# Second attention of a two-layer block: another order of the steps on TensorE, over three rotating pairs of banks

## Chip, cores and metric

The kernel runs on one core of one Trainium2 chip. The metric is the time of one execution on the device, in microseconds; smaller is better.

## What is computed

The reference chains two layers over an image tensor of 2 x 256 x 32 x 32 in float32. The first is a deformable attention with a position bias from a small network, an output projection and a two-layer network with GELU. The second, the one that matters here, is a plain attention of 8 heads of 32 channels over the N = 1024 pixels of each of the 2 images:

```python
xf = jnp.transpose(x.reshape(B, C, N), (0, 2, 1))
qkv = (xf @ W_qkv + b_qkv).reshape(B, N, N_HEADS, 3 * D_K)
q, k, v = jnp.split(qkv, 3, axis=-1)
attn = jnp.einsum('bihd,bjhd->bijh', q, k) * SCALE
attn = jax.nn.softmax(attn, axis=2)            # over j
res = jnp.einsum('bijh,bjhd->bihd', attn, v).reshape(B, N, N_HEADS * D_K)
res = res @ W_out + b_out + xf
```

## The kernel before

Five engine programs run side by side and meet by semaphores that count finished steps. The last fifth of the span is the second layer. It has G = 16 heads (two images of eight) and each head has NK = 8 tiles of 128 pixels, so there are SLOTS = 128 units. A unit goes through these steps:

- `along(x)` (L1041 to L1056, matmuls at L1055) on TensorE: the scores of 128 queries against all 1024 keys, queries on the partitions. Two matmuls of 512 columns fill one pair of PSUM banks. VectorE's `maxes(x)` (L760) takes the maximum of each query from it; `mx_ready` counts these.
- `turn(n)` (L1066): when the eight maxima of head n are there, one transpose lays them along the free axis. ScalarE (L572) and VectorE (L765) split the result in a high and a low part (`m_hi`, `m_lo`), and SP moves them by DMA (L330) as two more rows of the queries (`m_in`).
- `across(s)` (matmuls at L1083): the scores again, keys on the partitions and with the maximum subtracted by the two extra rows. It fills another pair of banks. ScalarE takes the exponential of it (L588) into one of six buffers; `pr_ready` counts these, `st_ready` the finished `across`.
- `weigh(s)` (L1094): the weighted sum of the values, in column-tiled matmuls of 32 columns of weights each, four side by side, into bank 6 or 7.
- GpSimd (L434) adds the exponentials of two units; `sums(j)` (L1104) sums such a pair over the partitions with column-tiled matmuls. `added` and `sums_done` count these.
- VectorE inverts the sums (L774, four pieces of a head) and divides (L782); SP places the head (L338).

`along` runs AHEAD_MAX = 14 units ahead of `across`: iteration s of the mixed loop has `along(s + 14)`. Three heads of queries and keys are held (HEADS3). The queries of head n + 3 are requested by ScalarE (L551) behind the exponential of unit 8n + 7, the last that reads that buffer, and `along` waits for them in `st_in` at its first tile. The keys are requested by SP (L324) at the same point.

`across(s)`, `along(x)` and `turn(n)` share six banks as three pairs, and a writer may only start when the pair's last reader is done. The functions `along_pair`, `turn_pair` and `across_pair` say which pair a step takes; `turned(x)` counts the transposes that stand before unit x, since each takes a turn in the rotation, and `turning(x)` says that one stands right there. `x` is always the unit of `along`, `s` that of `across`, x = s + 14.

In the mixed loop the order of one iteration before is

```python
if turning(x): turn(turned(x) - 1)
along(x); across(s); weigh(s - 2)
if s % 2 == 1 and s >= 5: sums((s - 5) // 2)
```

so two units are along, across, weigh, along, across, weigh, sums. The first 14 `along` stand ahead of the loop, among the projections of the values, and the last 14 iterations have none: those are called the tail. Behind the loop come the output projection and the stores.

Of the kernel before, what the change touches and what calls it, by code (L numbers as in the profile page):

```python
# [13 lines left out]
G = B * NH  # L14
# [8 lines left out]
NK = N // P  # L23
# [20 lines left out]
HEADS3, PRING, AHEAD_MAX = 3, 6, 14  # L44
# [3 lines left out]
SLOTS = G * NK  # L48
# [11 lines left out]
def build(nc, d, out):  # L60
# [5 lines left out]
    with ctx:  # L66
# [3 lines left out]
        def sem(name):  # L70
            return ctx.enter_context(nc.semaphore(name))
# [82 lines left out]
        def bank(i, n=1):  # L154
            return ps[:, 512 * i:512 * (i + n)]
# [5 lines left out]
        def v(name, i=0, n=1):  # L161
# [35 lines left out]
        tr_ready, m_hi, m_lo, m_in, ones_ready, bo_ready, bo_saved = (  # L197
            sem(x) for x in ("tr_ready", "m_hi", "m_lo", "m_in", "ones_ready", "bo_ready", "bo_saved"))
        sc_ready, mx_ready, st_ready, pr_ready, pv_done, o_done = (
            sem(x) for x in ("sc_ready", "mx_ready", "st_ready", "pr_ready", "pv_done", "o_done"))  # L200
# [20 lines left out]
        TURN = NK + TURN_LAG  # L221

        def turning(x):

            return TURN <= x < TURN + SLOTS and (x - TURN) % NK == 0

        def turned(x):

            return min(max((x - TURN) // NK + 1, 0), G)

        def along_pair(x):

            return (x + turned(x)) % 2 if x < AHEAD_MAX else (2 * (x - AHEAD_MAX) + turned(x) - 1) % 3

        def turn_pair(n):

            x = TURN + NK * n
            return x % 2 if x < AHEAD_MAX else (2 * (x - AHEAD_MAX) + n - 1) % 3

        def across_pair(s):  # L240

            return (2 * s + turned(s + AHEAD_MAX)) % 3

        block = ctx.enter_context(nc.Block())

# [192 lines left out]
        def _(act):  # L438
# [142 lines left out]
            for s in range(SLOTS):  # L581
                if turning(s + AHEAD_MAX):
                    max_high(turned(s + AHEAD_MAX) - 1)
                act.wait_ge(st_ready, s + 1)
                if s >= PRING:
                    act.wait_ge(pv_done, s - PRING + 1)
                    act.wait_ge(added, (s - PRING) // 2 + 1)
                act.activation(PT[s % PRING], bank(2 * across_pair(s), 2), ACT.Exp).then_inc(pr_ready, 1)  # L588
                if s % NK == NK - 1 and HEADS3 <= s // NK + 3 < G:
                    load_queries(s // NK + 3)  # L590
# [3 lines left out]
        def _(dve):  # L594
# [159 lines left out]
            def maxes(x):  # L754

                n, it = x // NK, x % NK
                dve.wait_ge(sc_ready, x + 1)
                if it == 0 and n >= HEADS3:
                    dve.wait_ge(tr_ready, n - HEADS3 + 1)
                dve.tensor_reduce(amax[n % HEADS3][:, it:it + 1], bank(2 * along_pair(x), 2), AX.X, ALU.max, negate=True).then_inc(mx_ready, 1)  # L760
# [51 lines left out]
        def _(pe):  # L812
# [98 lines left out]
            for m in range(PAIRS * G + AHEADQ):  # L911
# [7 lines left out]
                n = m - AHEADQ + 1  # L919
# [58 lines left out]
            for n in range(T):  # L978
                b, hf = n // 2, n % 2
                for ct in range(CT):  # L980
                    r = CT * n + ct
# [8 lines left out]
            for n in range(T):  # L990
                b, hf = n // 2, n % 2
                pe.wait_ge(xn2_ready, CT * (n + 1))
                for f in range(FT):
                    r = FT * n + f
# [6 lines left out]
                for ct in range(CT):  # L1001
                    r = CT * n + ct
# [38 lines left out]
            def along(x):  # L1041

                n, it = x // NK, x % NK
                if it == 0:
                    pe.wait_ge(st_in[n % HEADS3], 96 * (n // HEADS3 + 1))
                if 2 <= x < AHEAD_MAX and not turning(x - 1):
                    pe.wait_ge(mx_ready, x if turning(x) else x - 1)
                elif turning(x) or x == AHEAD_MAX:
                    pe.wait_ge(mx_ready, x)
                elif turning(x - 1):  # L1050
                    pe.wait_ge(m_lo, turned(x))
                elif x >= AHEAD_MAX + 2:
                    pe.wait_ge(pr_ready, x - AHEAD_MAX - 1)
                for hf in range(2):
                    last = pe.matmul(bank(2 * along_pair(x) + hf), QS[n % HEADS3][0:ROWS, P * it:P * (it + 1)],  # L1055
                                     KS[n % HEADS3][0:ROWS, HALF * hf:HALF * (hf + 1)], start=True, stop=True)  # L1056
                last.then_inc(sc_ready, 1)

            def turn(n):

                pe.wait_ge(mx_ready, NK * (n + 1))
                if n > 0:
                    pe.wait_ge(pr_ready, TURN + NK * n - AHEAD_MAX - 1)
                else:
                    pe.wait_ge(mx_ready, TURN - 1)
                pe.transpose(bank(2 * turn_pair(n))[0:NK, 0:P], amax[n % HEADS3][:, :], ident[:, :]).then_inc(tr_ready, 1)  # L1066

            def across(s):

                n, kt = s // NK, s % NK  # L1070
                if kt == 0:
                    pe.wait_ge(m_in, 32 * (n + 1))
                x = s + AHEAD_MAX
                if turning(x):
                    pe.wait_ge(pr_ready, s)
                elif x <= SLOTS:
                    pe.wait_ge(mx_ready, x - (s == 0))
                else:
                    pe.wait_ge(pr_ready, s - 2)
                    if x - 2 == TURN + NK * (G - 1):  # L1080
                        pe.wait_ge(m_lo, G)
                for hf in range(2):
                    last = pe.matmul(bank(2 * across_pair(s) + hf), KS[n % HEADS3][0:ROWS + 2, P * kt:P * (kt + 1)],  # L1083
                                     QS[n % HEADS3][0:ROWS + 2, HALF * hf:HALF * (hf + 1)], start=True, stop=True)
                last.then_inc(st_ready, 1)

            def weigh(s):

                n, kt = s // NK, s % NK
                if kt == 0 and n >= 2:  # L1090
                    pe.wait_ge(o_done, n - 1)
                pe.wait_ge(pr_ready, s + 1)
                for c in range(4):
                    last = pe.matmul(bank(6 + n % 2)[D * c:D * (c + 1), 0:QUARTER], V[:, n, kt, :],  # L1094
                                     PT[s % PRING][:, QUARTER * c:QUARTER * (c + 1)],
                                     start=(kt == 0), stop=(kt == NK - 1), skip_group_check=True)
                last.then_inc(pv_done, 1)

            def sums(j):

                n = j // (NK // 2)
                pe.wait_ge(added, j + 1)
                for c in range(4):
                    last = pe.matmul(bank(6 + n % 2)[D * c:D * (c + 1), QUARTER:2 * QUARTER], ones[:, :],  # L1104
                                     PSUMS[j % 2][:, QUARTER * c:QUARTER * (c + 1)],
                                     start=False, stop=(j % (NK // 2) == NK // 2 - 1), skip_group_check=True)
                last.then_inc(sums_done, 1)
# [3 lines left out]
            for n in range(2 * NK):  # L1111
                value(n)
                x = n - 2
                if turning(x):
                    turn(0)
                if x >= 0:
                    along(x)
            pe.wait_ge(vv_saved, 2 * NK)
            pe.wait_ge(ones_ready, 1 + HEADS3)
            for s in range(SLOTS + 4):  # L1120
                x = s + AHEAD_MAX
                if turning(x):
                    turn(turned(x) - 1)
                if x < SLOTS:
                    along(x)
                if s < SLOTS:
                    across(s)
                if 0 <= s - 2 < SLOTS:
                    weigh(s - 2)
                if s % 2 == 1 and s >= 5:  # L1130
                    sums((s - 5) // 2)

            pe.wait_ge(mx_ready, SLOTS)
            pe.wait_ge(pr_ready, SLOTS)
# [70 lines left out]
```

## Time and profile before

| | us |
|---|---|
| median of 3 runs | 1362.77 (1358.43 to 1364.05) |
| profiled execution | 1364.95 |
| its span | 1363.2 |
| TensorE busy | 1258.7 (92%) |
| VectorE busy | 807.5 (59%) |
| ScalarE busy | 815.0 (60%) |
| GpSimd busy | 694.4 (51%) |

The rows of the trace are those of one profiled execution. A row of the timeline gives the start of an instruction from the start of the span, its duration, engine, source line, operation, output and input; equal instructions that follow each other are merged (x8). PE is TensorE's matmuls, PEld its weight loads, DVE is VectorE, ACT ScalarE, POOL GpSimd, SPq and ACTq the DMA issues of SP and ScalarE. In square brackets stands the idle time of the engine before the row and what ended it. Ends of matmuls are modelled, so the distances between starts are the safer reading.

### The profile page before, as it was taken

How to read it: one execution, taken by the hardware profiler on the slowest of the kernel's cores; microseconds unless marked ns; L12 is line 12 of the kernel's file. 1: busy time of each engine (PE TensorE's matmuls, PEld its weight loads, DVE VectorE, ACT ScalarE, POOL GpSimd, SP SyncE). 2: the span in 40 equal slices, each digit the busy share in tenths (PEclk: the TensorE clock that was granted, in tenths of full speed). 3: DMA queues.
4: the chain of work that ended last, by engine and by line, in shares of the span. 5: the costliest groups of instructions: out<-in, count | busy, mean ns of one | idle time of the engine just before them, and what ended most of it. 6: DMA issues, size and time to landing. Idle time of an engine off the chain costs nothing.

```text
span 1363.2 us, 24765 instructions
## 1 busy us (share of the span) xinstructions
PE 1258.7 (92%) x10364; PEld 484.7 (36%) x10364; DVE 807.5 (59%) x954; ACT 815.0 (60%) x899; POOL 694.4 (51%) x363
## 2 busy tenths in 40 slices
PE   4159999999999999999999999879999899999998
PEld 2132222222222222222222223634444644444443
DVE  6876666666666666666666665730002667777773
ACT  3378777777777777777777775442212344555552
POOL 4076666666666666666666663320000055565564
PEclk9579999999999999999999999989999989999999
DMA  2141101110110011011101100000005222222212
GB/s 71 41 148 32 32 1 32 32 32 2 32 32 21 13 32 32 2 32 32 32 1 32 32 1 1 1 0 0 0 0 206 110 49 54 58 57 56 56 33 74
DMA packets 21842, 51.40 MB, mean 38 GB/s; under 512 B 5394, under 2 KB 10258, under 8 KB 21572
## 3 DMA queue, kind: packets, MB, share of 16 engines
q1 hardware_dynamic: 19424, 43.53, 11.9%
q10 hardware_dynamic: 2308, 6.30, 1.8%
q8 instruction: 82, 1.34, 0.4%
q14 instruction: 28, 0.23, 0.1%
HBM read 36.63 MB, written 10.95 MB: 35 GB/s over the span
## 4 chain that ended last, share of the span: by engine, by line
PE 85%; DMA 5%; DVE 4%; POOL 2%; ACT 2%; issue 1%; ACTq 1%; SPq 0%; POOLq 0%; DVEq 0%
PE ps L892 32%; PE ps L901 17%; PE ps L883 5%; PE ps L1055 5%; PE ps L998 4%; PE ps L1008 4%; PE ps L1083 4%; PE ps L1094 4%; DMA h1h<-q_d 3%; DVE big L636 2%; PE ps L1027 2%; DMA qk<-q_d 1%; PE ps L1104 1%; POOL big L394 1%; PE ps L1037 1%; PE ps L985 1%
## 5 line engine op out<-in xcount | busy, mean ns | idle before, releaser
L892 PE MATMUL ps<-big,w 64*64 64x512 f32 x4096 | 483.3, 588 | 0.0
L503 ACT ACTIVATE big<-ps 128x1024 f32<-128x1024 f32 x256 | 262.1, 1024 | 178.7 <-PE ps L892 178.7
L690 DVE TENSOR_SCALAR big<-big 128x1024 f32<-128x1024 f32 x256 | 177.8, 695 | 263.8 <-POOL big L409 263.8
L684 DVE TENSOR_TENSOR big<-qpad,ps 128x1024 f32<-128x1024 f32 x256 | 311.1, 1215 | 7.9 <-ACT ps L482 5.4
L409 POOL TENSOR_TENSOR big<-qpad 128x1024 f32<-128x1024 f32 x128 | 244.7, 1911 | 133.1 <-PE ps L892 69.4
L409 POOL TENSOR_TENSOR big<-qpad,V 128x1024 f32<-128x1024 f32 x128 | 244.5, 1910 | 129.6 <-PE ps L892 73.4
L503 ACT ACTIVATE big<-ps,vec 128x1024 f32<-128x1024 f32 x256 | 284.1, 1110 | 0.0
L901 PE MATMUL ps<-big,w3s 128*32 128x512 f32 x2048 | 246.2, 598 | 1.3 <-ACT big L503 1.3
L892 PEld LDWEIGHTS ps<-big,w 64*64 64x64 f32 x4096 | 146.5, 133 | 205.9 <-issue 112.6
L588 ACT ACTIVATE big<-ps 128x1024 f32<-128x1024 f32 x128 | 131.1, 1024 | 117.3 <-PE ps L1083 117.2
L434 POOL TENSOR_TENSOR big<-big 128x1024 f32<-128x1024 f32 x32 | 76.1, 2378 | 232.0 <-ACT big L588 232.0
L760 DVE TENSOR_REDUCE amax<-ps 128x1 f32<-128x1024 f32 x128 | 156.4, 1222 | 59.7 <-PE ps L1055 56.0
L901 PEld LDWEIGHTS ps<-big,w3s 128*32 128x32 f32 x2048 | 53.4, 109 | 181.8 <-ACT big L503 92.2
L434 POOL TENSOR_TENSOR BT<-big 128x1024 f32<-128x1024 f32 x32 | 76.3, 2383 | 59.5 <-ACT big L588 49.6
L883 PE MATMUL ps<-S,wl 57*64 57x512 bf16 x1024 | 102.1, 389 | 1.5 <-ACT vs L498 1.5
L1094 PE MATMUL ps<-big 128*32 128x256 f32 x1024 | 82.9, 397 | 0.0
L883 PEld LDWEIGHTS ps<-S,wl 57*64 57x64 bf16 x1024 | 29.5, 105 | 144.7 <-ACT big L503 80.7
L1055 PE MATMUL ps<-h1l,h1h 96*128 96x512 f32 x176 | 67.0, 463 | 10.9 <-DMA h1h<-q_d 9.1
L752 DVE SCALAR_TENSOR_TENSOR X<-ps,vec,X 128x512 f32<-128x512 f32 x8 | 6.0, 751 | 105.0 <-PE ps L1008 105.0
L544 ACT ACTIVATE big<-ps,vec 128x512 f32<-128x512 f32 x32 | 22.0, 689 | 73.0 <-PE ps L998 73.0
L1083 PE MATMUL ps<-h1h,h1l 98*128 98x512 f32 x176 | 57.2, 406 | 0.4 <-DVE amax L760 0.4
L998 PE MATMUL ps<-XN,m 128*128 128x512 f32 x128 | 55.7, 593 | 0.8 <-DVE X L743 0.8
(146 smaller groups left out, 988.4 us busy)
## 6 DMA issues: line engine op xcount, KB each, us to landing
raw<-s_f SPq DMA_DIRECT2D x32, 512.0 KB, 6.2
h1l<-k_d SPq DMA_DIRECT2D x33, 128.0 KB, 3.6
h1h<-q_d ACTq DMA_DIRECT2D x33, 128.0 KB, 4.1
X<-in_x SPq DMA_DIRECT2D x2, 1024.0 KB, 6.1
q_d<-XN SPq DMA_DIRECT2D x4, 512.0 KB, 3.6
k_d<-XN SPq DMA_DIRECT2D x4, 512.0 KB, 4.1
q_d<-big SPq DMA_DIRECT2D x4, 512.0 KB, 4.0
k_d<-big SPq DMA_DIRECT2D x4, 512.0 KB, 5.3
```

What stands on the lines that cost most here:

```text
L409: pool.tensor_tensor(h1[m % HRING].rearrange("p (y a b) -> p y a b", y=2, b=W), u.unsqueeze(2).to_broadcast(shape), a[:, :, HALF // W * hf ...
L434: pool.tensor_tensor(PSUMS[j % 2], PT[2 * j % PRING], PT[(2 * j + 1) % PRING], ALU.add).then_inc(added, 1)
L503: act.activation(h2[m % H2RING], z2[m % ZRING], ACT.Relu, bias=v("cb2") if m % 2 else 0.0).then_inc(h2_ready, 1)
L588: act.activation(PT[s % PRING], bank(2 * across_pair(s), 2), ACT.Exp).then_inc(pr_ready, 1)
L684: dve.tensor_tensor(h1[m % HRING].rearrange("p (y a b) -> p y a b", y=2, b=W), u.unsqueeze(2).to_broadcast(shape), b[:, :, HALF // W * hf: ...
L690: dve.tensor_scalar(h1[m % HRING], h1[m % HRING], 0.0, None, ALU.max).then_inc(h1_ready, 1)
L760: dve.tensor_reduce(amax[n % HEADS3][:, it:it + 1], bank(2 * along_pair(x), 2), AX.X, ALU.max, negate=True).then_inc(mx_ready, 1)
L883: pe.matmul(z2[m % ZRING][CH * y:CH * (y + 1), HALF * x:HALF * (x + 1)], wl1[CH * x:CH * x + KROWS, 2 * w + y, :], S[CH * x:CH * x + KROWS ...
L892: last = pe.matmul(z2[m % ZRING][CH * y:CH * (y + 1), HALF * x:HALF * (x + 1)], w2[CH * x:CH * (x + 1), :], h1[m % HRING][CH * x:CH * (x + ...
L901: last = pe.matmul(zb[32 * k:32 * (k + 1), :], w3s[:, a:a + 32], h2[(m + k // 2) % H2RING][:, HALF * (k % 2):HALF * (k % 2 + 1)], start=(m ...
L1055: last = pe.matmul(bank(2 * along_pair(x) + hf), QS[n % HEADS3][0:ROWS, P * it:P * (it + 1)], KS[n % HEADS3][0:ROWS, HALF * hf:HALF * (hf ...
L1094: last = pe.matmul(bank(6 + n % 2)[D * c:D * (c + 1), 0:QUARTER], V[:, n, kt, :], PT[s % PRING][:, QUARTER * c:QUARTER * (c + 1)], start=( ...
```

## The change

On TensorE the mixed loop runs in rounds of two units. A round is across, along, across, along, then both weighs of the round before, then the sums of the round before that. `across` now stands ahead of `along` in each unit, and the transpose ahead of both. The rotation over the three pairs follows the new order: the steps of a round take pairs c - 1, c, c + 1 and c + 2, which is c - 1 again. The waits in `along`, `turn` and `across` are rewritten to fit; the matmuls, the buffers, and the programs of the other four engines stay as they are, but for the pair from which they read.

```diff
         def along_pair(x):
 
-            return (x + turned(x)) % 2 if x < AHEAD_MAX else (2 * (x - AHEAD_MAX) + turned(x) - 1) % 3
+            if x < AHEAD_MAX:
+                return (x + turned(x)) % 2
+            s = x - AHEAD_MAX
+            return (4 * (s // 2) + 2 * (s % 2) + turned(x)) % 3
...
         def across_pair(s):
 
-            return (2 * s + turned(s + AHEAD_MAX)) % 3
+            return (4 * (s // 2) + 2 * (s % 2) + turned(s + AHEAD_MAX) - 1) % 3
...
                 if 2 <= x < AHEAD_MAX and not turning(x - 1):
                     pe.wait_ge(mx_ready, x if turning(x) else x - 1)
-                elif turning(x) or x == AHEAD_MAX:
+                elif 2 <= x < AHEAD_MAX:
+                    pe.wait_ge(m_lo, 1)
+                elif x < 2:
+                    pass
+                elif turning(x):
                     pe.wait_ge(mx_ready, x)
-                elif turning(x - 1):
-                    pe.wait_ge(m_lo, turned(x))
-                elif x >= AHEAD_MAX + 2:
-                    pe.wait_ge(pr_ready, x - AHEAD_MAX - 1)
+                elif x == AHEAD_MAX:
+                    pe.wait_ge(mx_ready, x - 1)
+                else:
+                    pe.wait_ge(pr_ready, x - AHEAD_MAX)
...
                 pe.wait_ge(mx_ready, NK * (n + 1))
-                if n > 0:
-                    pe.wait_ge(pr_ready, TURN + NK * n - AHEAD_MAX - 1)
+                if n < G - 1:
+                    pe.wait_ge(mx_ready, TURN + NK * n - 1)
                 else:
-                    pe.wait_ge(mx_ready, TURN - 1)
+                    pe.wait_ge(pr_ready, TURN + NK * n - AHEAD_MAX - 2)
...
                 if turning(x):
                     pe.wait_ge(pr_ready, s)
-                elif x <= SLOTS:
-                    pe.wait_ge(mx_ready, x - (s == 0))
-                else:
+                elif turning(x - 1):
+                    pe.wait_ge(m_lo, turned(x))
+                elif s == 0:
+                    pe.wait_ge(mx_ready, AHEAD_MAX)
+                elif s > 1 and x - 1 <= SLOTS:
+                    pe.wait_ge(mx_ready, x - 1)
+                elif s > 1:
                     pe.wait_ge(pr_ready, s - 2)
-                    if x - 2 == TURN + NK * (G - 1):
-                        pe.wait_ge(m_lo, G)
...
-            for s in range(SLOTS + 4):
-                x = s + AHEAD_MAX
-                if turning(x):
-                    turn(turned(x) - 1)
-                if x < SLOTS:
-                    along(x)
-                if s < SLOTS:
-                    across(s)
-                if 0 <= s - 2 < SLOTS:
-                    weigh(s - 2)
-                if s % 2 == 1 and s >= 5:
-                    sums((s - 5) // 2)
+            for r in range(SLOTS // 2 + 2):
+                for s in (2 * r, 2 * r + 1):
+                    x = s + AHEAD_MAX
+                    if turning(x):
+                        turn(turned(x) - 1)
+                    if s < SLOTS:
+                        across(s)
+                    if x < SLOTS:
+                        along(x)
+                if 0 < r <= SLOTS // 2:
+                    weigh(2 * r - 2)
+                    weigh(2 * r - 1)
+                if r >= 2:
+                    sums(r - 2)
```

## Rows read from the trace of the kernel before

**Rows 1.** Busy time by engine, with granted clock, DMA share, rate: mixed loop with `along`.

```profile
core 0: us, PE busy (x) PEld busy (x) DVE busy (x) ACT busy (x) POOL busy (x), PEclk, DMA share, GB/s
1086.45:1322.26 235.81, 222.10 (x1807) 110.91 (x1807) 170.63 (x193) 120.28 (x128) 133.33 (x56) 0.98 0.23 52
```

**Rows 2.** Timeline, two units in the middle of the loop.

```profile
1216.78 0.73 PE L1055 MATMUL ps<-h1l,h1h 96*128 96x512 f32 x2
...
1217.36 0.63 PE L1083 MATMUL ps<-h1h,h1l 98*128 98x512 f32 x2
1217.55 1.22 DVE L760 TENSOR_REDUCE amax<-ps 128x1 f32<-128x1024 f32 x1 [0.44 <-PE ps L1055]
...
1217.91 0.64 PE L1094 MATMUL ps<-big 128*32 128x256 f32 x8
...
1218.48 0.73 PE L1055 MATMUL ps<-h1l,h1h 96*128 96x512 f32 x2
1218.70 0.55 DVE L774 RECIPROCAL big<-ps 128x64 f32<-128x64 f32 x1
...
1220.06 0.61 PE L1104 MATMUL ps<-BT,ones 128*32 128x256 f32 x8
...
1220.61 0.73 PE L1055 MATMUL ps<-h1l,h1h 96*128 96x512 f32 x2
```

**Rows 3.** Waits, 1090 to 1322: who waited for whom, total us, times, longest.

```profile
PE ps L1055 <- DMA h1h<-q_d: 9.1, 9, 1.6
...
PE ps L1055 <- DMA qk<-q_d: 4.1, 4, 1.2
```

**Rows 4.** Busy time of two stretches, columns as in rows 1.

```profile
1107.20:1114.00 6.80, 6.80 (x34) 3.13 (x33) 3.01 (x4) 2.32 (x3) 1.66 (x1) 0.50 0.00 0
1127.70:1131.10 3.40, 3.40 (x24) 1.72 (x20) 1.48 (x2) 1.55 (x2) 0.00 (x0) 0.51 0.00 0
```

**Rows 5.** Timeline, the third pair of units, and the tail.

```profile
1092.90 0.73 PE L1055 MATMUL ps<-qk 96*128 96x512 f32 x2
...
1323.49 0.73 PE L1083 MATMUL ps<-qk 98*128 98x512 f32 x2
...
1324.15 0.64 PE L1094 MATMUL ps<-big 128*32 128x256 f32 x8
1324.26 1.02 ACT L588 ACTIVATE big<-ps 128x1024 f32<-128x1024 f32 x1 [0.20 <-PE ps L1083]
...
1342.59 1.05 PE L1094 MATMUL ps<-big 128*32 128x256 f32 x16
...
1343.45 0.61 PE L1104 MATMUL ps<-big,ones 128*32 128x256 f32 x8
```

**Rows 6.** Timeline, steps that had to wait, and what released them.

```profile
1088.49 0.73 PE L1083 MATMUL ps<-h1h,h1l 98*128 98x512 f32 x2 [0.39 <-DVE amax L760]
...
1089.06 0.62 PE L1055 MATMUL ps<-qk 96*128 96x512 f32 x2
...
1211.59 1.23 DVE L760 TENSOR_REDUCE amax<-ps 128x1 f32<-128x1024 f32 x1 [0.49 <-PE ps L1055]
...
1212.96 0.08 PEld L1066 LDWEIGHTS ps<-ident,amax 128*8 128x8 f32 x1 [0.41 <-DVE amax L760]
...
1341.81 1.02 ACT L588 ACTIVATE big<-ps 128x1024 f32<-128x1024 f32 x1 [0.21 <-PE ps L1083]
...
1342.88 0.27 PEld L1094 LDWEIGHTS ps<-big 128*32 128x32 f32 x8 [0.16 <-ACT big L588]
```

**Rows 7.** Timeline, requests of queries and the `along` that waited for them.

```profile
1099.66 1.31 ACTq L551 DMA_DIRECT2D h1h<-q_d  x3
...
1106.08 0.73 PE L1055 MATMUL ps<-h1l,h1h 96*128 96x512 f32 x2 [1.64 <-DMA h1h<-q_d]
...
1125.97 0.73 PE L1055 MATMUL ps<-h1l,h1h 96*128 96x512 f32 x2 [1.45 <-DMA h1h<-q_d]
...
1203.56 1.30 ACTq L551 DMA_DIRECT2D h1h<-q_d  x3
...
1209.10 0.74 PE L1055 MATMUL ps<-h1l,h1h 96*128 96x512 f32 x2 [0.76 <-DMA h1h<-q_d]
```

## Prediction

> **What bounds the kernel now.** I first cut the span into stages. The change touches only the second attention, from the first step of its mixed loop to the end of the loop. [Rows 1] gives the part in which `along` still runs, 235.81 us: TensorE is busy 222.10 us, VectorE 170.63, ScalarE 120.28, GpSimd 133.33. So TensorE is the candidate, and the timeline of two units shows how it spends its time [rows 2]: `along` at 1216.78, `across` at 1217.36, `weigh` at 1217.91, `along` at 1218.48, `across` 0.57 later, and after the second `weigh` the `sums` at 1220.06 and the next `along` at 1220.61. Each step starts about 0.57 us after the one before, sums 0.45 and the step after sums 0.55; two units take 1220.61 - 1216.78 = 3.83 us, with nothing idle. TensorE's own order of instructions is the limit there.
>
> Then the waits of that stretch [rows 3]: `along` waited 13 times, once for each head from the fourth on, for the DMA of its queries, 9.1 + 4.1 = 13.2 us of idle TensorE. Third, the granted clock [rows 4]: two stretches, 6.8 us and 3.4 us long, at 0.50 and 0.51, that is at 1.2 GHz instead of 2.4. Each begins one to two microseconds after one of the two longest DMA waits, and the clock was 2.4 GHz before it.
>
> These close the account: first two rounds 1092.90 - 1086.45 = 6.45 us [rows 1, 5], then 55 rounds x 3.83 = 210.65, DMA waits 13.2, together 230.3; measured 235.8. The remaining 5.5 us is the low clock, half of its 10.2 us or 5.1, and 0.4 for getting under way after the waits. After 1322.26 seven rounds without `along` remain.
>
> **Part 1: the order on TensorE.** The same matmuls are issued; only their neighbours change. Rows show what a neighbour is worth. A pair of 512-column matmuls that stands alone between column-tiled groups takes 1324.15 - 1323.49 = 0.66 us [rows 5]; two pairs together take 1217.91 - 1216.78 = 1.13 [rows 2], which is 0.47 for the second. So a run of full-width matmuls pays 0.19 once. For `weigh` and `sums`: alone 0.57 [rows 2], one after another 0.43 (two weighs and then the sums, 1343.45 - 1342.59 = 0.86 for two) [rows 5]: 0.14 once per run. Before, two units hold two runs of each kind; after, one of each. Four pairs take 1.13 + 2 x 0.47 = 2.07, weigh, weigh and sums 0.45 + 0.43 + 0.55 = 1.43, the round 3.50. Against 3.83 this would be 0.33 less, if nothing waits.
>
> The Trainium skill, "TensorEngine Tiling (Array Packing)", Tiling Modes, says that a change of tiling mode drains the engine; it gives no price. The rows above give it, 0.19 + 0.14 = 0.33 for a run of each kind.
>
> **Part 2: the wait that it adds.** Three pairs of banks now serve four writers in a round, so the second `along` takes the pair that the first `across` of the same round has just filled: it waits until ScalarE has exponentiated it (pr_ready at s + 1). Before, `along` needed only the exponential of two units back. From the start of a first-in-run `across`, the exponential starts at 1324.26 - 1323.49 = 0.77 [rows 5] and takes 1.02; the trace has no `along` that waits for it, so I bound the wake-up by the nearest rows [rows 6]: weights for ScalarE's result start at 1342.88, 0.05 after 1341.81 + 1.02; the transpose starts 0.14 after VectorE's 1211.59 + 1.23. I take 0.05, the row with the same engine pair. So the second `along` starts at 0.77 + 1.02 + 0.05 = 1.84, where TensorE would have reached it at 0.57 + 2 x 0.47 = 1.51: a stall of 0.33. After a wait the run begins anew: at 1088.49 `across` was released by VectorE and the next step came 0.57 later, not 0.47 [rows 6]; so this `along` costs the full 0.66. Queued behind it are both weighs, the sums and the next `across`. The round is 1.84 + 0.66 + 1.43 = **3.93 us**, 0.10 more than before: the wait eats all that the order gives. 55 rounds: **+5.5 us** (with 0.14 for the wake-up +10.5; with the weight load hidden, -0.1 a round, 0).
>
> That last end has a page too. The Trainium skill, "TensorE: Matmul & The Clock Gate", Architectural detail, says the queue can pull weight loads ahead of matmuls in flight. By that the sum would be some 5 us lower. The 0.57 at 1088.49 speaks against it where the load itself carries the wait.
>
> Nobody else becomes late. A maximum starts 0.77 after a first-in-run `along` [rows 2], 0.10 less further in the run, as there the weights are loaded beforehand. The first of a round starts at 1.24 and ends at 2.47; a reciprocal of 0.55 [rows 2] may follow; the second ends by 4.25, and the third step of the next round, at 4.97, is the first that needs it. The second exponential runs from 1.80, when ScalarE is free, to near 2.87; the sum on GpSimd, which is busy 133 us of the 236, has more than a round from there until `sums` reads it, as before.
>
> **Part 3: the DMA wait.** The queries of head n+3 are issued when exponential 8n+7 starts: 1203.56, and `along` could go at 1209.10, 5.5 us; in the worst case 1099.66 to 1106.08, 6.4 [rows 7]. Before, that issue came 0.89 before the end of a round (0.67 into the last `across`, which starts at 1218.48 + 0.57 = 1219.05, 1.56 before 1220.61) and the `along` opened the round after the next one: 0.89 + 3.83 = 4.7 us, short by 0.8 to 1.7. Now `across` of unit 8n+7 is third in its round and its exponential starts when the previous one ends, at 1.80; the `along` is second in the round after next, at 2 x 3.93 + 0.57 = 8.4. There are 6.6 us for a transfer of 5.5 to 6.4. The wait goes in all 13 places: **-13.2 us**, and -0.4 for the restarts. Next late there is nothing: the keys go out on SP at the same moment, behind the move of the maxima; `across` of a new head comes 0.3 us earlier after its transpose (7.9 for 8.2), and two rounds of only 2.9 in the tail of before passed with no DMA wait.
>
> **Part 4: the clock.** Both low stretches follow waits of 1.64 and 1.45 us [rows 7]; after the 11 others, (13.2 - 3.1) / 11 = 0.9 us each, there is none. With these gone I take the clock back: **-5.1 us**; if not, up to 5.1 stays.
>
> **Part 5: start and tail.** At the start `across` goes first and waits for the same maximum as `along` did; following the same durations round 2 begins 0.4 us earlier. `across` now stands before `along` behind m_in, but the first head's maxima leave some 6 us before. Tail: seven rounds of 1.13 + 1.43 = 2.56 instead of 0.66 + 0.57 + 0.66 + 1.00 = 2.89: -2.3; the last transpose's `across` waits there for the exponential just before it (ends at 2.87 of a 2.56 round): +0.4. Together **-2.3**.
>
> **Sum.** +5.5 - 13.2 - 0.4 - 5.1 - 2.3 = -15.5. The profiled execution took 1364.95 (span 1363.2), so 1349.4; it lies 2.2 above the median of the runs, 1362.77. The prediction is 1362.8 - 15.5 = **1347.3 us**.
>
> **Rivals.**
> 1. *The bubble turns the clock down (slower).* The new stall of 0.33 us stands in every round, where the old one came once a head. If 15 stretches of 3.4 us at 1.2 GHz follow, half of that or 1.7 us each, that adds 26 to the 5.1 not saved: 1347.3 + 5.1 + 26 = 1378. It passes +0.5% (1369.6) from 11 stretches on. Against it: TensorE would idle 0.33 of 3.93 us, 8%; a round with one of the 11 shorter DMA waits idled 0.9 of 4.8, 19%, and kept its clock [rows 2 to 4]. Chance 0.06. The Trainium skill, "TensorE: Matmul & The Clock Gate", A second HAM failure mode, describes just this: short idling between groups that cycle through PSUM banks makes the clock swing. The present trace has no such case.
> 2. *The DMA wait stays.* If the queries' landing hangs on something that moves with the loop (contention, the keys), 13.6 us stay: about 1361. For it: landing varies, 5.5 to 6.4, with 0.2 to spare in the worst case. Chance 0.06.
> 3. *The exponential's wait costs nothing*, because the pair is free earlier than the records say: rounds of 3.50, 55 x 0.43 = 24 us less: 1323. Against it: in [rows 6] the waiting instruction starts after its releaser's record ends. Chance 0.04.
> 4. *The forecast*, 0.84. Its own ends: weight load hidden, -5.5, 1342; wake-up 0.14 and half the clock loss kept, +5 + 2.6, 1355.
>
> **Range** 1338 to 1359, which holds the forecast with its ends and leaves out most of the rivals, some 0.17. Half a per cent, about what a measurement of this kernel can tell from no change, is 6.8 us: faster means below 1356. Nearly all of case 4 and case 3: 0.84; same, rival 2 and the upper edge of 4: 0.10; slower, rival 1: 0.06.
>
> **What the profile would show.** A round of 3.93 us with `along` in it, the second `along` released by ScalarE with 0.3 us idle or a little more, 57 times; no DMA row among TensorE's waits; a granted clock of 1.00 from 1090 on. Wrong would be: rounds of 3.5 (rival 3), a clock below 1.00 in many stretches (1), DMA waits at the heads (2), or a maximum of VectorE as the releaser of `across`, which my account says never comes.

## The result and the profile after

The changed kernel takes 1348.93 us (median of 6 runs, 1347.46 to 1351.33) against 1361.4 us for the kernel before (6 runs, 1357.19 to 1364.05); the ratio is 0.9908 with a 95% interval of 0.9887 to 0.9928, that is 9.8 to 15.4 us less. The forecast was 1347.3. The profiled execution took 1349.23 us, its span is 1347.4, against 1364.95 and 1363.2 before. It is faster by more than half a per cent, and by the mechanism forecast; one term, that of the clock, was too large.

The chain that ended last, first before, then after (share of the span by engine):

```profile
PE 85%; DMA 5%; DVE 4%; POOL 2%; ACT 2%; issue 1%; ACTq 1%; SPq 0%; POOLq 0%; DVEq 0%
```

```profile
PE 86%; ACT 6%; DVE 4%; POOL 2%; issue 1%; DMA 1%; ACTq 0%; SPq 0%; POOLq 0%; DVEq 0%
```

DMA has all but left the chain and ScalarE has come in: one wait was exchanged for another. The next rows give the busy time by engine, with granted clock, DMA share and rate, of the mixed loop with `along` (it answers to rows 1), and then of the tail up to the output projection:

```profile
core 0: us, PE busy (x) PEld busy (x) DVE busy (x) ACT busy (x) POOL busy (x), PEclk, DMA share, GB/s
1085.69:1308.56 222.87, 212.61 (x1806) 113.69 (x1806) 166.70 (x193) 115.44 (x128) 133.52 (x56) 1.00 0.24 55
1308.56:1330.20 21.64, 20.34 (x234) 10.39 (x230) 4.62 (x11) 13.85 (x15) 19.05 (x8) 1.00 0.08 20
```

The loop fell from 235.81 to 222.87 us, 12.9 less, at a granted clock of 1.00 throughout. The tail fell by 2.0, from 1345.92 - 1322.26 = 23.66 to 21.64. Another 0.8 us lies before the loop, where nothing was changed.

One round of two units after (it answers to rows 2; lines 1062, 1092, 1103 and 1113 are `along`, `across`, `weigh` and `sums`):

```profile
1206.06 0.73 PE L1092 MATMUL ps<-h1h,h1l 98*128 98x512 f32 x2
...
1206.62 0.64 PE L1062 MATMUL ps<-h1l,h1h 96*128 96x512 f32 x2
1206.82 1.97 ACT L591 ACTIVATE big<-ps 128x1024 f32<-128x1024 f32 x2 [1.99 <-PE ps L1092]
...
1207.10 0.63 PE L1092 MATMUL ps<-h1h,h1l 98*128 98x512 f32 x2
...
1207.77 1.30 ACTq L554 DMA_DIRECT2D h1h<-q_d  x3
...
1207.90 0.73 PE L1062 MATMUL ps<-h1l,h1h 96*128 96x512 f32 x2 [0.17 <-ACT big L591]
...
1208.56 1.07 PE L1103 MATMUL ps<-big 128*32 128x256 f32 x16
...
1209.45 0.61 PE L1113 MATMUL ps<-BT,ones 128*32 128x256 f32 x8
...
1209.99 0.73 PE L1092 MATMUL ps<-qk 98*128 98x512 f32 x2
```

The round is 1209.99 - 1206.06 = 3.93 us. Counted from its start, the exponential starts at 0.76, the second `along` at 1.84, the weighs at 2.50, the sums at 3.39. The waits of TensorE over the loop were these (who waited for whom, total us, times, longest; it answers to rows 3):

```profile
PE ps L1062 <- ACT big L591: 9.9, 55, 0.2
PE ps L1092 <- DVE amax L763: 0.2, 1, 0.2
```

No DMA is among them. The 13 waits for queries are gone, and 55 short ones for the exponential stand instead. They show as 0.17 us each, because the modelled end of the matmul before hides the rest of the gap: against the 1.51 at which TensorE would have reached the step without a wait, the delay is 1.84 - 1.51 = 0.33.

### The profile page after: what moved, and what is told of

Read it like the earlier page. It is cut to its first block, busy times and chain, and to the rows that moved or that the text cites. A ratio compares the mean times of both kernels' runs of the same rounds, so it can differ in the third digit from the quotient of the medians.

```text
span 1347.4 us, 24764 instructions
## 1 busy us (share of the span) xinstructions
PE 1246.8 (93%) x10364; PEld 488.4 (36%) x10364; DVE 803.2 (60%) x954; ACT 808.8 (60%) x899; POOL 694.1 (52%) x363
## 4 chain that ended last, share of the span: by engine, by line
PE 86%; ACT 6%; DVE 4%; POOL 2%; issue 1%; DMA 1%; ACTq 0%; SPq 0%; POOLq 0%; DVEq 0%
PE ps L895 33%; PE ps L904 18%; PE ps L886 5%; PE ps L1103 5%; ACT big L591 4%; PE ps L1001 4%; PE ps L1011 4%; PE ps L1062 4%; PE ps L1092 3%; DVE big L639 2%; PE ps L1113 2%; PE ps L1030 2%; POOL big L397 1%; PE ps L1040 1%; PE ps L988 1%; PE ps L1154 1%
## 5 line engine op out<-in xcount | busy, mean ns | idle before, releaser
L506 ACT ACTIVATE big<-ps 128x1024 f32<-128x1024 f32 x256 | 262.0, 1023 | 179.1 <-PE ps L895 179.1
L591 ACT ACTIVATE big<-ps 128x1024 f32<-128x1024 f32 x128 | 125.3, 1024 | 91.7 <-PE ps L1092 91.7
L1062 PE MATMUL ps<-h1l,h1h 96*128 96x512 f32 x176 | 62.5, 437 | 6.9 <-ACT big L591 6.6
L1103 PE MATMUL ps<-big 128*32 128x256 f32 x1024 | 68.5, 385 | 0.0
```

Of the source, the lines that this page charges most:

```text
L506: act.activation(h2[m % H2RING], z2[m % ZRING], ACT.Relu, bias=v("cb2") if m % 2 else 0.0).then_inc(h2_ready, 1)
```

## The experiments

Times are medians; ratios are against the kernel before on the same chip, with 95% intervals. "Loop" is the time from the first matmul of the first `across` to the last matmul of the last `along`, read from the starts in the timeline. It leaves out the stages before and after, which vary by several us from run to run (over all the profiles the loop begins between 1085.3 and 1092.1 us). It is 233.4 us in the kernel before and 221.1 in the kernel after.

### Without the loads: what the DMA waits were worth

```diff
-                if HEADS3 <= n + 2 < G:
-                    sp.wait_ge(st_ready, NK * (n + 2 - HEADS3 + 1))
-                    load_keys(n + 2)
...
-                if s % NK == NK - 1 and HEADS3 <= s // NK + 3 < G:
-                    load_queries(s // NK + 3)
...
-                    pe.wait_ge(st_in[n % HEADS3], 96 * (n // HEADS3 + 1))
+                    pe.wait_ge(st_in[n % HEADS3], 96)
```

> The kernel before, with the loads of queries and keys from the fourth head on left out: later heads compute with the first three heads' data, so part of the computation is changed; the order on TensorE and every other wait stay. My theory says the DMA waits (13.2 us idle, 0.4 of restarts) and the low clock that follows the two longest (up to 5.1) went with the change: rounds stay at 3.83 us, the waits and the two low stretches vanish, 1343 to 1348 us. Rival, the gain came from the order of the matmuls and not from the DMA waits: 1358 to 1361.

Measured 1347.92 us, ratio 0.9885 (0.9853 to 0.9917), loop 217.2 us. Without its loads the old order is as fast as the new order with them. So the gain of the change is, on balance, the vanished DMA wait, not the order of the matmuls: in the loop the old order is even 3.9 us ahead (217.2 against 221.1), and the new one makes good 2.0 of that in the tail. Low clock was expected to be gone, but the 217.2 us hold one stretch of it at the start, where `along` and `across` wait for VectorE.

```profile
1088.00:1305.24 217.24, 216.86 (x1786) 109.11 (x1785) 169.01 (x192) 119.26 (x127) 132.88 (x56) 0.98 0.04 9
1090.00:1096.80 6.80, 6.80 (x28) 3.30 (x28) 3.16 (x4) 3.34 (x4) 3.02 (x2) 0.50 0.00 0
```

```profile
1087.46 0.70 PE L1050 MATMUL ps<-h1l,h1h 96*128 96x512 f32 x2 [1.41 <-DVE amax L755]
...
1089.48 0.79 PE L1078 MATMUL ps<-h1h,h1l 98*128 98x512 f32 x2 [0.38 <-DVE amax L755]
```

The wait of 1.41 us stands at the start of the loop in nine other traces too, the kernels before and after among them, and no low clock follows it in those.

### The critical exponential made shorter, and longer

```diff
-                act.activation(PT[s % PRING], bank(2 * across_pair(s), 2), ACT.Exp).then_inc(pr_ready, 1)
+                cols = N if s % 2 else HALF
+                act.activation(PT[s % PRING][:, 0:cols], bank(2 * across_pair(s), 2)[:, 0:cols], ACT.Exp).then_inc(pr_ready, 1)
```

> The kernel after, with the exponential of every even unit over the first 512 of its 1024 columns only (the other half of its weights is left out of the computation as such, old values stand there). My theory: the second along waits for exactly this exponential; shortened by some 0.4 us it ends at about 0.77 + 0.6 + 0.05 = 1.42 into the round, before TensorE wants the pair at 1.51, and the round falls from 3.93 to 3.50 us: 24 us less, about 1325. Rival, the order is worth less than the rows say and something else bounds the round (VectorE's maxima, GpSimd's sums): 1340 to 1349.

Measured 1328.19 us, ratio 0.9737 (0.9700 to 0.9773); loop 198.8, which is 22.3 us less than the kernel after, where 24 were expected. The median is 3 us above the 1325 expected. The loop accounts for 1.7 of them; the rest lies outside it (in this profile, of an execution of 1331.0, the loop began at 1089.8, 4 us later than in that of the kernel after). The timeline:

```profile
1205.95 0.73 PE L1093 MATMUL ps<-qk 98*128 98x512 f32 x2
...
1206.72 0.60 ACT L592 ACTIVATE big<-ps 128x512 f32<-128x512 f32 x1 [1.55 <-PE ps L1093]
...
1207.44 0.66 PE L1063 MATMUL ps<-h1l,h1h 96*128 96x512 f32 x2
...
1208.03 1.07 PE L1104 MATMUL ps<-big 128*32 128x256 f32 x16
...
1209.46 0.27 PE L1074 MATMUL ps<-ident,amax 128*8 128x128 f32 x1
```

The exponential is over at 1.37 of the round, the second `along` starts at 1.49 without a wait, and the next round (here with a transpose) begins after 3.51 us. That is the round of pure TensorE work, 3.50 in the prediction; neither VectorE nor GpSimd holds it up here.

The other way round:

```diff
+        spare, spared = sb("spare", [P, D]), sem("spared")
...
+                if s % 2 == 0:
+                    act.wait_ge(spared, s // 2)
+                    act.activation(spare[:, :], ident[:, 0:D], ACT.Exp).then_inc(spared, 1)
                 act.activation(PT[s % PRING], bank(2 * across_pair(s), 2), ACT.Exp).then_inc(pr_ready, 1)
```

> The kernel after, with one small activation (32 columns, some 0.1 to 0.25 us, read from the trace) put before the exponential of every even unit; nothing is left out. My theory: the round's chain is across, exponential, along, so each round with along grows by the whole of it: 57 times, +6 to +14 us, round 4.05 to 4.2. Rival, the exponential's wait is slack that something else fills: under +2 us.

```profile
1207.34 0.23 ACT L594 ACTIVATE spare<-ident 128x32 f32<-128x32 f32 x1 [0.20 <-PE ps L1096]
1207.48 1.92 ACT L595 ACTIVATE big<-ps 128x1024 f32<-128x1024 f32 x2
...
1208.54 0.73 PE L1066 MATMUL ps<-h1l,h1h 96*128 96x512 f32 x2 [0.30 <-ACT big L595]
```

Measured 1356.97 us, ratio 0.9944 (0.9922 to 0.9966); loop 227.7, 6.6 us more than the kernel after. The small activation pushes the exponential back by 0.14 (1207.34 to 1207.48), not by its own 0.23, since the two overlap; TensorE's wait grows from 0.17 to 0.30. 57 x 0.13 = 7.4 us against 6.6 in the loop, inside the 6 to 14 expected. The chain is as drawn, and there is no slack in it.

### The kernel before once more: how steady is the clock?

> The kernel before, unchanged, profiled once more. My theory: the DMA waits of about 1 us stand again at each head from the fourth on; whether the two stretches of low clock come again is open. If they are absent the time should be some 5 us lower, near the fastest runs of before (1357 to 1359); if they stand, 1362 to 1365.

Measured 1362.93 us, with 13 DMA waits again (13.6 us in all), loop 230.8. Of low clock there is one stretch instead of two:

```profile
1239.90:1243.30 3.40, 3.40 (x24) 1.76 (x20) 1.57 (x2) 1.64 (x2) 0.00 (x0) 0.50 0.00 0
```

It follows the one wait of 1.58 us; the twelve others were 0.81 to 1.38. So the low clock in this loop differs between runs of one kernel: 10.2 us in the first profile, 3.4 in this one. The loop is 2.6 us shorter than in the first profile and the profiled execution 2.0 us (1362.93 against 1364.95), so the stages outside it vary by as much as what was looked for. The executions without a trace point the same way: on one chip the kernel before ran 17 times, and the granted clock, averaged over the whole execution, goes with the time, from 0.976 in the fastest (1356.81 us) to 0.970 in the slowest (1364.63). In which stage their low clock lay is not recorded.

### Who stands first in the round

The kernel of this run makes its order of steps from a list; written in the loop of the kernel after, the change is:

```diff
-                    if s < SLOTS:
-                        across(s)
                     if x < SLOTS:
                         along(x)
+                    if s < SLOTS:
+                        across(s)
```

The three pairs go round in the order of the steps, and each step waits for the reader of the step three before it.

> Rounds of two units as in the kernel after, but along first: along, across, along, across, two weighs, sums, pairs and waits fitted. Nothing is left out. My theory: the fourth step takes the first step's pair, whose reader is now VectorE's maximum, 0.77 + 1.23 + 0.05 = 2.05 after the round's start instead of 1.84: round 2.05 + 0.66 + 1.43 = 4.14, 55 x 0.21 = 11.5 us more than the kernel after; the queries have some 5.5 us for 5.5 to 6.4, so DMA waits of 0 to 0.9 return, up to 12 us: 1360 to 1372. Rival, only the number of runs of each tiling mode counts, not who stands first: 1349.

Measured 1364.5 us, ratio 1.0017 (0.9997 to 1.0036), loop 234.7.

```profile
1204.52 0.73 PE L1126 MATMUL ps<-qk 96*128 96x512 f32 x2
...
1206.56 0.73 PE L1145 MATMUL ps<-h1h,h1l 98*128 98x512 f32 x2 [0.40 <-DVE amax L827]
1207.22 1.07 PE L1159 MATMUL ps<-big 128*32 128x256 f32 x16
```

The fourth step starts at 2.04 (forecast 2.05), released by VectorE. The matmuls are the same and stand in runs of the same length, yet the loop is 13.6 us longer than in the kernel after. That comes from which reader frees the pair of the fourth step, the exponential or the maximum (55 x 0.21 = 11.5), and from small DMA waits that return (6, 2.1 us in all). Rounds of two units by themselves give nothing.

### The same gain with one constant

AHEAD_MAX is 13 instead of 14 in the kernel before. The pairs and waits are derived from the order of the steps.

> The order of the kernel before (rounds of one unit, along first), with along 13 instead of 14 units ahead of across, and nothing left out. One unit more between the request of the queries and their use is 1.7 us, more than every wait seen but none above it. My theory: the DMA waits go, as in the run without the loads, at rounds of 3.83 us: 1346 to 1350, the whole gain of the change with a single constant. Rival, the shorter lead brings a wait for the moved maxima (5.4 us instead of 7.1 from transpose to across): 1355 to 1362.

Measured 1351.1 us, ratio 0.9918 (0.9892 to 0.9943), loop 221.4: about the kernel after's time, with the old order, and 1.1 us above what was expected. All DMA waits are gone and `across` never waits for the moved maxima. But the rounds with a transpose take 4.18 us instead of 3.84. The transpose now stands in the second unit of a round, with no `sums` ahead of it, and the `along` behind it takes the pair of the `along` before and waits for its maximum. It starts 0.36 after the transpose instead of 0.03:

```profile
1205.77 1.23 DVE L827 TENSOR_REDUCE amax<-ps 128x1 f32<-128x1024 f32 x1 [0.90 <-PE ps L1126]
...
1206.70 0.08 PEld L1136 LDWEIGHTS ps<-ident,amax 128*8 128x8 f32 x1 [0.41 <-issue]
...
1207.05 0.30 PEld L1126 LDWEIGHTS ps<-h1l,h1h 96*128 96x128 f32 x2 [0.27 <-DVE amax L827]
```

### How long the queries really take

```diff
-                if s % NK == NK - 1 and HEADS3 <= s // NK + 3 < G:
-                    load_queries(s // NK + 3)
+                if s % NK == 0 and s > 0 and HEADS3 <= s // NK + 2 < G:
+                    load_queries(s // NK + 2)
```

> The kernel after, with the queries of a head requested one exponential later (behind that of unit 8n+8 instead of 8n+7), nothing left out. My theory: 6.6 us of slack become 3.7, so the DMA wait comes back at 13 heads with 1.8 to 2.7 us each, 23 to 35 us; and waits as long as the two that were followed by a low clock are now the rule, so several stretches at 1.2 GHz, up to 1.7 us each, up to 22 us: 1372 to 1400. Rival for the clock, the low stretches have nothing to do with the wait's length: none or one or two in the loop, and 1372 to 1384.

Measured 1353.73 us in one run, with a loop of 221.1 us, the same as the kernel after to 0.1 us, and no DMA wait at all. My expectation failed. The timeline has the request of the queries at 1215.30, and the `along` that needs them, at 1219.03, follows the `across` at 1218.46 without a gap, 3.7 us after the request. The median time from an issue to its landing tells why. First the kernel before, then this one:

```profile
h1l<-k_d SPq DMA_DIRECT2D x27, 128.0 KB, 3.6
h1h<-q_d ACTq DMA_DIRECT2D x27, 128.0 KB, 4.1
```

```profile
h1l<-k_d SPq DMA_DIRECT2D x27, 128.0 KB, 2.6
h1h<-q_d ACTq DMA_DIRECT2D x27, 128.0 KB, 2.6
```

In the kernels before and after, the keys and queries of a head, three transfers of 128 KB each, are requested in the same moment from two queues and slow each other; here the keys go out 3.0 us ahead (1212.27). I tried this on the kernel before, by asking for the keys one `across` later:

```diff
-                    sp.wait_ge(st_ready, NK * (n + 2 - HEADS3 + 1))
+                    sp.wait_ge(st_ready, NK * (n + 2 - HEADS3 + 1) + 1)
```

> The kernel before, with the keys requested one across (1.7 us) later than the queries; nothing is left out. My theory after the run with late queries: keys and queries that are requested together slow each other from about 3.4 to 5.5 us until usable; apart, the queries are there after 3.4 and the keys 1.7 + 3.4 = 5.1 us after the same moment, with 4.7 available: waits of 0.4 instead of 1.0 us, 6 to 8 us less, 1353 to 1357. Rival, no contention, a transfer takes its 5.5 us whatever else runs: waits of 2.5 us, 20 us more and the low clock on top, 1380 and above.

Measured 1361.19 us, ratio 1.0005 (0.9990 to 1.0020), loop 229.4, waits 10.8 us instead of 13.2.

```profile
1200.68 1.25 ACTq L551 DMA_DIRECT2D h1h<-q_d  x3
...
1202.80 1.24 SPq L324 DMA_DIRECT2D h1l<-k_d  x3
...
1206.22 0.30 PEld L1055 LDWEIGHTS ps<-h1l,h1h 96*128 96x128 f32 x2 [1.24 <-DMA h1l<-k_d]
```

The mechanism holds, the gain does not, and the time is outside the 1353 to 1357 expected. Apart, the keys are usable 3.4 us after their request (1206.22 - 1202.80). But the next `across` comes 2.12 us later, not the 1.7 that I had taken, for a `sums` stands between; 2.12 + 3.4 is the same 5.5 as together. A transfer that took 5.5 us by itself would have made waits of some 3 us. The longest wait, 1.58 us at 1106.27, is again followed by 6.8 us at 1.2 GHz (1107.0 to 1113.8), against 10.2 us of low clock in the first profile of the kernel before; with the 2.4 us of waits that makes the 4.0 by which the loop is shorter.

### Long waits and the clock

Here the condition of the request is `s % NK == 2 and s > NK`, so that it goes out in the very round that needs the queries.

> The kernel after, with the queries requested behind the exponential of unit 8n+10, whose start is in the same round as the along that needs them; nothing is left out. In the run with the request one exponential late the transfer took 3.5 us or less from request to use. So TensorE must wait 0.77 + 3.4 - 0.57 = 3.6 us at each of 13 heads: 47 us. My theory of the clock (long waits are followed by 1.2 GHz): low stretches after most of these waits, 13 x 1.7 us or more, together 1410 to 1440. Rival (the low stretches of before were chance): none or one or two, 1394 to 1400.

Measured 1425.18 us in one run, loop 290.7. TensorE's waits, and three of the stretches of low clock that go with them:

```profile
PE ps L1062 <- DMA h1h<-q_d: 32.2, 9, 3.7
PE ps L1062 <- DMA qk<-q_d: 14.5, 4, 3.8
```

```profile
1113.10:1119.90 6.80, 5.86 (x32) 3.09 (x33) 2.45 (x2) 1.02 (x1) 0.03 (x1) 0.50 0.00 1
1137.00:1140.40 3.40, 3.40 (x27) 1.23 (x25) 2.12 (x2) 1.02 (x1) 0.00 (x0) 0.50 0.00 0
1345.20:1352.00 6.80, 6.80 (x34) 3.84 (x35) 2.73 (x3) 1.39 (x3) 1.12 (x1) 0.50 0.00 0
```

The waits add 46.7 us, as expected. Each of the 13 is attended by a fall to 1.2 GHz, four times for 6.8 us and nine times for 3.4, 57.8 us in all. Half of that, 28.9, and the 46.7 make 75.6; the loop grew by 290.7 - 221.1 = 69.6. Two things are likely to make the difference: some stretches begin in the wait itself (that at 1113.1 ends up beside a matmul only at 1114.04), and 13 fewer waits for the exponential stand in the list. After waits of this length the low clock is no chance. For shorter waits chance has a part, as the stretch in the run without the loads shows.

### The exponential in two halves, one per bank

The run with the half exponential named the price of the new wait, 22 us. It can be had without leaving anything out: split each exponential by bank, and let each matmul of the next writer wait for its own bank. In short form (the waits of `weigh` and of the other engines count in halves accordingly):

```diff
-                act.wait_ge(st_ready, s + 1)
+                act.wait_ge(st_ready, 2 * s + 1)
...
+                for hf in range(2):
+                    if hf == 1:
+                        act.wait_ge(st_ready, 2 * s + 2)
+                    act.activation(PT[s % PRING][:, HALF * hf:HALF * (hf + 1)], bank(2 * across_pair(s) + hf), ACT.Exp).then_inc(pr_ready, 1)
...
                 for hf in range(2):
+                    pe.wait_ge(pr_ready, 2 * p[1] + 1 + hf)     # p[1]: the across that filled this pair
                     last = pe.matmul(bank(2 * along_pair(x) + hf), ...
```

> The order of the kernel after, but every exponential in two halves of 512 columns, the first started when the first matmul of across is done, and the second along's first matmul waits for the first half only, its second matmul for the second half. Nothing is left out. My theory: the stall of the second along shrinks from 0.43 us (0.33 and the 0.10 of a new start) to 0.1 to 0.2, though ScalarE works 2 x 0.60 instead of 1.02 us: round 3.6 to 3.7, 13 to 18 us less than the kernel after, 1331 to 1336. Rival, the halves cost as much as they release: 1345 to 1352.

Measured 1326.23 us, ratio 0.9742 (0.9701 to 0.9782), loop 200.0: 5 us below the range expected.

```profile
1209.25 0.74 PE L1148 MATMUL ps<-qk 98*128 98x512 f32 x2
...
1209.79 1.57 ACT L658 ACTIVATE big<-ps 128x512 f32<-128x512 f32 x3 [1.48 <-PE ps L1148]
...
1210.76 0.66 PE L1129 MATMUL ps<-h1l,h1h 96*128 96x512 f32 x2
...
1210.93 0.19 PEld L1129 LDWEIGHTS ps<-h1l,h1h 96*128 96x128 f32 x1 [0.21 <-ACT big L658]
...
1211.35 1.07 PE L1162 MATMUL ps<-big 128*32 128x256 f32 x16
...
1212.79 0.50 PE L1148 MATMUL ps<-h1h,h1l 98*128 98x512 f32 x1
```

The round is 3.54 us, 0.03 above the pure work. The first half starts at 0.54, 0.23 before a whole exponential could, and three halves take 1.57 us, so one follows another after 0.49 rather than 0.60. Only the weight load of the second matmul still waits, 0.21 us of its own idle time, nearly all beside the matmul in flight.

Then once more, beside the unchanged kernel after on the same chip:

> The kernel with split exponentials again, beside the kernel after on the same chip: 20 to 25 us less than it, 1324 to 1330, rounds of 3.54 us. Rival: the first measurement was a lucky chip; less than 10 us.

> The kernel after, unchanged, to have both versions on one chip: 1347 to 1351.

Measured 1330.01 us (ratio 0.9773, 0.9752 to 0.9793) against 1349.29 (ratio 0.9920, 0.9902 to 0.9939): 19 us less than the kernel after and 31 less than the kernel before. The loops are 200.7 and 221.1. I had said 20 to 25 less. The first run's better total comes for the most part from ahead of the loop, which began at 1085.3 in its profile and at 1087.3 in this one.

## Why the prediction was right, and where it was off

**Part 1, the order on TensorE.** Right. A round without stall is 3.51 us in the run with the half exponential (3.50 forecast). In the tail of the kernel after two `across` follow each other in one merged record, and the round to the next step, the transpose, is 1311.12 - 1308.56 = 2.56 (forecast 2.56):

```profile
1308.56 1.19 PE L1092 MATMUL ps<-qk 98*128 98x512 f32 x4
1309.69 1.07 PE L1103 MATMUL ps<-big 128*32 128x256 f32 x16
1310.58 0.61 PE L1113 MATMUL ps<-BT,ones 128*32 128x256 f32 x8
1311.12 0.27 PE L1073 MATMUL ps<-ident,amax 128*8 128x128 f32 x1
```

So the price of the runs, 0.19 + 0.14, was read rightly from rows of the old order. The Trainium skill, "TensorEngine Tiling (Array Packing)", Tiling Modes, leaves it open.

**Part 2, the added wait.** Right in place and size: 1.84 and 3.93 in the trace. From the start of round 2 at 1091.68 there are 216.9 us to the tail, 3.94 for each of 55 rounds. The rounds without a transpose take 3.934 in the mean, so the term is 55 x 0.104 = +5.7 (+5.5 forecast); another 0.5 us is in the 14 rounds that hold a transpose. The bound that I chose for the wake-up (0.05, not 0.14) was the right one, and the weight load of the waiting `along` was not hidden: it starts with its matmul, and the weighs follow after the full 0.66. The Trainium skill, "TensorE: Matmul & The Clock Gate", Architectural detail, says that the queue can pull weight loads ahead of matmuls in flight; for the load that carries this wait no run shows it. The runs with a shorter and a longer exponential and with `along` first show cause and price. One thing the prediction said would never come did come, once and early: the `across` at 1089.55 was released by a maximum of VectorE, with 0.17 us idle.

**Part 3, the DMA wait.** Right in effect: 13 waits gone, -13.2 us. The run without the loads confirms that this carries the gain. But the step "a transfer of 5.5 to 6.4" was read as a property of the transfer. It is what two simultaneous requests make of one that takes 3.4 to 3.7 until usable. Here that changed nothing, since keys and queries are still requested together and 6.6 us suffice; it misled the expectation of the run with late queries by 18 us and more (1353.73 against 1372 to 1400). Rival 2 named the contention with the keys, which is real, but it is the same in both orders: the median landing of a transfer of queries is 4.1 us before and 4.2 after.

**Part 4, the clock.** The mechanism holds, the size is the term that was off. I took all 5.1 us of one profile. A second profile of the same kernel has 3.4 us of low clock in the loop, which is 1.7 us of time. With 1.7 the forecast would be -12.1; the medians differ by 12.5. That this term is what was off is likely, not shown, as the low clock in the loop is known of profiled executions alone. The profiled pair, by contrast, has 12.9 in the loop and 2.0 in the tail, near the forecast's 15.5, because that profile of the kernel before had two such stretches. That the time came within 1.6 us of the forecast, while the gain was 3.0 us off, is luck: with three more runs the median of the kernel before fell by 1.4 us, from 1362.77 to 1361.4.

**Part 5.** Start: the first two rounds took 1091.68 - 1085.69 = 5.99 instead of 6.45, -0.46 (-0.4 forecast). Tail: -2.0 (-1.9 with the +0.4 for the last transpose).

**Rival 1, the bubble that turns the clock down,** did not come: 55 stalls of 0.33 us stood in a loop with a granted clock of 1.00, here, in the kernel after once more and in the run with late queries. The Trainium skill, "TensorE: Matmul & The Clock Gate", A second HAM failure mode, describes such a swing for groups that cycle through PSUM banks; no run of this order shows it. What does lower the clock is the single long wait: it fell at 13 of 13 DMA waits of 3.4 to 3.8 us, in some before the wait was over, and in the two profiles of the kernel before and in the run with later keys it fell after all four of 1.45 to 1.64 us and after none of the shorter ones (0.6 to 1.4). The one stretch that follows shorter waits, 1.41 and 0.38 us for VectorE, is in the run without the loads. **Rival 3** needed rounds of 3.50; they came only when the exponential was cut or split.

## What to carry to other kernels

Merging equal steps into longer runs pays only if the buffers turn round as fast as the run: compute, for the last writer of a run, when its buffer's reader is done. Here the order's 0.33 us a round went into a wait that costs 0.43 (0.33 of delay and 0.10 for the new start), and the gain came from a side effect, a load that had 6.6 us instead of 4.7 to arrive, which one constant would have brought too. When a release is the bound, make it finer before changing the order again: splitting the reader by bank was worth more than the whole change.

## What the runs showed of the hardware that I had not expected

- Two groups of three 128 KB loads requested together from SP and ScalarE have both landed after 5.5 to 6.4 us. Requested 2 us or more apart, each group has landed after 3.2 to 3.7, a few only after 3.8 to 4.5. The median landing of one transfer falls from 4.1 (queries) and 3.6 (keys) to 2.6 us.
- Short activations overlap: two exponentials of 1024 columns, 1.02 us each, take 1.97 together, and halves of 0.60 follow one another after 0.49. So splitting costs ScalarE little, and it lets the first half start 0.23 us earlier.
- After a DMA wait of 1.45 to 1.64 us TensorE's clock was at 1.2 GHz for 3.4 or 6.8 us in four of four cases. Taken as half of the stretch, that costs as much again as the wait, or twice as much. After a wait of 1.41 us for VectorE it was so in one of ten traces. The time of a removed wait of that length is therefore not always only its own.
